# Last expert stage: one list per expert and choice, row weights in the tiles, and scatters that add to the output

## What is computed

```
x = x + L1_gnn(layernorm(x))                 # called x3 below
xf = layernorm(x).reshape(-1, 128)           # 8192 rows
top_w, top_i = top_k(xf @ Wg + bg, 2)
top_w = softmax(top_w)                       # 1/(1+e), e/(1+e) with e = exp(second - first)
for e in range(8):
    h = gelu(xf @ W1[e] + b1[e])             # 128 -> 512
    out += w_dense[:, e] * (h @ W2[e] + b2[e])
x = x + out
```

## Time and profile before

| quantity | us |
|---|---|
| three runs | 1516.81, 1512.54, 1510.47 |
| their median | 1512.54 |
| span of the profiled execution, first to last instruction | 1509.3 |
| phase_gnn1 with its barriers, about | 912 to 1188 |
| last expert stage, first transpose to last result | 1188.1 to 1457.5 |
| phase_finish, with the barrier before it | 1459 to 1509.3 |

### The profile page before, as it was taken

How to read it: one execution, slowest core, us unless ns; L and a number is a source line. 1 busy time by engine, 2 the same in 40 slices (tenths; PEclk the granted TensorE clock), 3 DMA queues, 4 the chain that set the end, 5 groups by cost and what they waited for, 6 DMA issues and landing times. The chain is left out here.

```text
span 1509.3 us, 31426 instructions
## 1 busy us (share of the span) xinstructions
PE 1158.0 (77%) x8464; PEld 980.3 (65%) x8464; DVE 935.4 (62%) x3451; ACT 727.7 (48%) x1776; POOL 772.8 (51%) x767
## 2 busy tenths in 40 slices
PE   5888888767888871799999983677762499999940
PEld 3666566557787761588888872555552389999930
DVE  3788888998888963355555554888865022222228
ACT  5777777537667751233333332544441245555520
POOL 3466666642666777344444441177776355555520
PEclk9999999979989985799999996988885699999985
DMA  7100000000011113466666662032212477777759
GB/s 186 22 2 2 2 1 2 2 1 1 30 33 36 35 44 89 145 197 196 195 193 193 194 194 88 29 99 69 68 43 71 142 223 228 229 228 227 225 168 288
DMA packets 133627, 166.82 MB, mean 111 GB/s; under 512 B 17328, under 2 KB 105136, under 8 KB 133520
## 3 DMA queue, kind: packets, MB, share of 16 engines
q1 hardware_dynamic: 99344, 122.30, 27.9%
q0 software_dynamic: 16832, 34.77, 6.5%
q10 hardware_dynamic: 17344, 8.49, 2.0%
HBM read 122.31 MB, written 43.19 MB: 110 GB/s over the span
## 5 line engine op out<-in xcount | busy, mean ns | idle before, releaser
L1879 POOL DMA_INDIRECT rows<-m_yb,m_dsti x270 | 258.7, 958 | 316.1 <-DVE m_dsti L2029 272.5
L1965 ACT ACTIVATE m_sg<-psum 128x256 f32<-128x256 f32 (+3 forms) x216 | 79.8, 370 | 179.1 <-PE psum L1909 132.9
L1110 POOL DMA_INDIRECT dispatch<-g_flat,g1r_pos x128 | 127.1, 993 | 58.0 <-issue 35.3
L1110 POOL DMA_INDIRECT dispatch<-common_v,a1r_pos x128 | 128.8, 1007 | 53.2 <-issue 40.2
L1909 PE MATMUL psum<-m_xT,m_w 128*128 128x256 f32 (+3 forms) x648 | 140.3, 366 | 0.7 <-ACT m_xT L1955 0.7
L1972 ACT ACTIVATE m_sg<-psum,m_w 128x256 f32<-128x256 f32 (+1 forms) x216 | 86.1, 458 | 93.9 <-PE psum L1914 93.2
L2011 DVE TENSOR_TENSOR m_hT<-psum,m_sg 128x256 f32<-128x256 f32 (+3 forms) x216 | 87.6, 407 | 62.4 <-ACT m_sg L1965 58.6
L1909 PEld LDWEIGHTS psum<-m_xT,m_w 128*128 128x128 f32 (+1 forms) x648 | 106.2, 178 | 18.3 <-ACT m_xT L1955 0.9
L1994 DVE TENSOR_TENSOR m_yb<-psum,m_w 128x256 f32<-128x256 f32 (+1 forms) x54 | 22.0, 407 | 144.8 <-PE psum L1924 144.8
L1924 PE MATMUL psum<-m_w,m_sg 128*128 128x128 f32 x808 | 99.2, 275 | 0.5 <-DVE m_yb L1994 0.5
L1914 PE MATMUL psum<-m_xT,m_w 128*128 128x256 f32 (+1 forms) x432 | 96.4, 366 | 0.5 <-ACT m_xT L1953 0.5
(11 more groups left out here) (273 smaller groups left out, 3056.1 us busy)
## 6 DMA issues: line engine op xcount, KB each, us to landing
m_w<-in_c_wall SPq DMA_DIRECT2D x54, 578.0 KB, 3.7
m_w<-in_c_wall SPq DMA_DIRECT2D x54, 533.0 KB, 3.5
m_xg<-dispatch SPq DMA_DIRECT2D x94, 130.0 KB, 3.6
ahead_w<-in_c_wall SPq DMA_DIRECT2D x18, 578.0 KB, 4.1
ahead_w<-in_c_wall SPq DMA_DIRECT2D x18, 533.0 KB, 4.5
g1c_y<-rows SPq DMA_DIRECT2D x32, 256.0 KB, 3.2
fin_y<-rows ACTq DMA_DIRECT2D x32, 256.0 KB, 6.4
rows<-m_yb,m_dsti POOLq DMA_INDIRECT x270, 3.3
```

The costliest lines, as they stand in the source:

```text
L1110: pool.indirect_dma_start(out=dest, out_offset=bass.IndirectOffsetOnAxis(ap=self.pos[t % 2][:, k, p:p + 1], axis=0), in_=flat[:, p, :], in ...
L1879: pool.indirect_dma_start(out=rows_out, out_offset=bass.IndirectOffsetOnAxis(ap=dsti[j][:, t:t + 1], axis=0), in_=yb[j][:, t, :], in_offse ...
L1965: act.activation(sg[j % 2][0:cn, k, 0:rows], up_banks[j % 2][k][0:cn, 0:rows], ACT.Silu)\
```

## The change

- The last mixture has 16 lists, one for each expert and choice, in two sets. The rank product, the positions, the base counts, the table and the tail fills have a leading dimension of 2. `Routing` and `Tables` get the new classes `SplitRouting` and `SplitTables` for this stage; the first mixture keeps the old ones.
- The number of tiles is fixed for each set: 31 full and 9 halves, so 80 tiles with 62 full and 18 halves in place of 72 with 63 and 9. All tiles of the first choice come first, then all of the second.
- ScalarE takes exp(second - first) once per batch inside the steps, writing it behind the row's id. `pool_scatter` waits for it. The key of the first expert is no longer written, the sum of both choices (`both`) no longer computed, and `vector_weights` no longer run for this stage.
- SP stores x3 to the output inside phase_gnn1, 16 stores of 256 KB, and waits for them at the stage's end. SP fills 16 list tails in place of 8, and 8 more spare tiles near the program's start.
- `phase_last` takes the place of the second `phase_experts` and of `phase_finish`. VectorE adds b2 and then multiplies each row by its weight; `yw_ready`, given by the second instruction, replaces `y_ready` for SP's loads and POOL's scatters. The scatter goes to the output with an add in the DMA. Before the first scatter of the second set POOL waits for all scatters of the first.
- The output tensor is longer by the place for the dummy rows; the host keeps the first 128 frames.

The diff, cut to its core:

```diff
+LISTS = 2 * (NE + 1)
+FULL_K = PAIRS * 128 // TILE - 1
+TILES_K = FULL_K + (PAIRS * 128 + NE * (HALF - 1)) // HALF - 2 * FULL_K
+OUT_FRAMES = FRAMES + TRASH // NODES
...
-            for rows in (list1, list2):
+            for rows, spare in ((list1, NE), (list2, NE), (list2, 2 * NE + 1)):
...
-        phase_experts(nc, banks, c, T, state2, list2, rows2, A["c_wall2"], False, "m2", x, None, None, ahead)
-        phase_finish(nc, x, state2, rows2, out_dram)
+        T2 = SplitTables(ctx, nc)
+        phase_gnn1(nc, W, x, banks, c, T2, state, rows1, list2, ahead, A["c_wall2"], out_dram)
+        phase_last(nc, banks, c, T2, list2, out_rows, A["c_wall2"], ahead)
...
+class SplitRouting:
...
+        r = self.ranks(bank)
+        pe.matmul(r[:, :, 0:PB, :], self.c["tri"][:, :], self.oh[:, :, :, :], start=True, stop=False, skip_group_check=True)
...
+    def scalar_exp(self, act, t, flat):
...
+        act.wait_ge(*self.d_ready.now(t))
+        act.activation(flat[:, :, C + 1], self.d[:, t % 2, :], ACT.Exp).then_inc(self.e_ready.sem, 1)
...
+    def pool_tag(self, pool, t, flat):
...
+        pool.wait_ge(*self.step.now(t, 0))
+        pool.tensor_copy(flat[:, :, C], self.c["ids"][:, bass.ds(t * PB, PB)]).then_inc(self.tagged.sem, 1)
...
+    def pool_scatter(self, pool, t, first, last, flat, dest):
...
+        pool.wait_ge(*self.pstep.now(t, 4))
+        pool.wait_ge(*self.e_ready.now(t))
+        pool.wait_ge(*self.tagged.now(t))
...
+class SplitTables:
...
+        sp.wait_ge(self.chain, 1)
+        for k in range(2):
+            for e in range(NE):
+                row = sp.value_load(self.tail[0:1, k, e:e + 1], min_val=0, max_val=(LISTS - 1) * CAP)
+                sp.dma_start(rows_in[bass.ds(row, TILE), :].rearrange("(t p) c -> p t c", t=2), nobody[:, 2 * e:2 * e + 2, :])\
+                  .then_inc(self.filled, 16)
...
                     mixed_out(g)
+                    if b % 2 == 1 and runs_batch(h - 1):
+                        R.scalar_exp(act, h - 1, flat[(h - 1) % 3])
                     head_h3(g + 1)
                 in_pairs(step)
-                R.scalar_exp(act, False)
...
-                turns(sp, 0, GROUPS // 2, lambda turn: M.fetch(sp, turn))
+                def store_x3(g):
+                    sp.wait_ge(*x3_ready.now(g))
+                    sp.dma_start(out_dram[:, PG * g:PG * g + PG, :], x[:, PG * g:PG * g + PG, :]).then_inc(x3_stored, 16)
+
+                for turn in range(GROUPS // 2):
+                    M.fetch(sp, turn)
+                    for g in range(2 * turn - 6, 2 * turn - 4):
+                        if g >= 0:
+                            store_x3(g)
+                for g in range(GROUPS - 6, GROUPS):
+                    store_x3(g)
                 T.sync(sp, c, dest)
                 ahead.sync(sp, "m2", T, R, wall, dest)
+                sp.wait_ge(x3_stored, 16 * GROUPS)
...
+def phase_last(nc, banks, c, T, rows_in, out_rows, wall, ahead):
...
+                    sp.wait_ge(*yw_ready.now(g, j - UN))
...
+                        pool.wait_ge(*yw_ready.now(g, j))
+                        pool.wait_ge(*share_ready.now(g, 4 * j + 3))
+                        pool.sem_inc(gate, 1)
+                        if isinstance(g, int) and g == SIDE and j == 0:
+                            for i in range(UN):
+                                pool.wait_ge(stored[i], sent(SIDE, i))
+                        for t in range(halves(g, j)):
+                            pool.indirect_dma_start(
+                                out=out_rows, out_offset=bass.IndirectOffsetOnAxis(ap=dsti[j][:, t:t + 1], axis=0),
+                                in_=yb[j][:, t, :], in_offset=None, compute_op=ALU.add).then_inc(stored[j], 16)
...
+                    dve.tensor_tensor(y, bY[:, 0:n * C].rearrange("r (t c) -> r t c", t=n),
+                                      bass.AP(b.tensor, b.offset, [b.ap[0], [0, n], [1, C]]), ALU.add).then_inc(y_ready.sem, 1)
+                    dve.wait_ge(*y_ready.now(g, j))
+                    dve.wait_ge(*share_ready.now(g, 4 * j + 2))
+                    dve.tensor_tensor(y, y, over_c(share[jj][:, 0:n], n), ALU.mult).then_inc(yw_ready.sem, 1)
...
+                    dve.tensor_scalar(total[j][:, 0:n], xg[j][:, 0:n, C + 1], 1.0, None, ALU.add).then_inc(sr.sem, 1)
+                    dve.wait_ge(*sr.now(g, 4 * j))
+                    dve.reciprocal(share[j][:, 0:n], total[j][:, 0:n]).then_inc(sr.sem, 1)
+                    if k == 1:
+                        dve.wait_ge(*sr.now(g, 4 * j + 1))
+                        dve.tensor_tensor(share[j][:, 0:n], share[j][:, 0:n], xg[j][:, 0:n, C + 1], ALU.mult).then_inc(sr.sem, 1)
+                    else:
+                        dve.sem_inc(sr.sem, 1)
+                    dve.tensor_copy(dsti[j][:, 0:n], xg[j][:, 0:n, C]).then_inc(sr.sem, 1)
```

More of the change, by code:

```diff
@@ L1804, in phase_experts @@
         sg = [sb(f"sg{i}", [128, NK, TILE]) for i in range(2)]
[L1805 removed]
+        hT = [sb(f"hT{i}", [128, NK, TILE]) for i in range(2)]
         dst = [sb(f"dst{i}", [128, 2]) for i in range(UN)]
@@ L2004, in body @@
                         rows = HALF * halves(g, j)
-                        if late is not None and adds:
+                        if adds:
                             late_add(g, j)
-                        if swiglu:
-                            for k, (c0, cn) in enumerate(chunks):
-                                dve.wait_ge(*act_done.now(g, NK * j + k))
-                                dve.wait_ge(*pe_down.now(g, j - 2))
-                                dve.tensor_tensor(hT[j % 2][0:cn, k, 0:rows], up_banks[j % 2][k][0:cn, TILE:TILE + rows],
-                                                  sg[j % 2][0:cn, k, 0:rows], ALU.mult).then_inc(h_ready.sem, 1)
+                        for k, (c0, cn) in enumerate(chunks):
+                            dve.wait_ge(*act_done.now(g, NK * j + k))
+                            dve.wait_ge(*pe_down.now(g, j - 2))
+                            dve.tensor_tensor(hT[j % 2][0:cn, k, 0:rows], up_banks[j % 2][k][0:cn, TILE:TILE + rows],
+                                              sg[j % 2][0:cn, k, 0:rows], ALU.mult).then_inc(h_ready.sem, 1)
                         if not (first and j == 0):
@@ L2418, in _ @@
                 in_pairs(step)
-                T.vector(dve, c, state2["base"], R.pstep.now(GROUPS // 2 - 1, 4))
-                R.vector_weights(dve, False)
+                T.vector(dve, c, R.pstep.now(GROUPS // 2 - 1, 4))
             @block.gpsimd
@@ L2464, in _ @@
             @block.vector
             def _(dve):
-                open_signals(dve, M.dve_signals)
-        with nc.Block() as block:
-            @block.scalar
-            def _(act):
-                M.fetch(act, 0)
-                turns(act, 1, GROUPS // DEPTH, lambda turn: M.fetch(act, turn))
-            @block.vector
-            def _(dve):
-                turns(dve, 0, GROUPS // DEPTH, lambda turn: [M.vector_mix(dve, turn * DEPTH + b, b, x) for b in range(DEPTH)])
-            @block.sync
-            def _(sp):
-                def body(g):
-                    sp.wait_ge(*M.mixed.now(g, 2 * PG - 1))
-                    sp.dma_start(out_dram[:, bass.ds(g * PG, PG), :], x[:, bass.ds(g * PG, PG), :]).then_inc(stored, 16)
-                turns(sp, 0, GROUPS, body)
-                sp.wait_ge(stored, 16 * GROUPS)
+                open_signals(dve, [y_ready, yw_ready, share_ready])
@@ L2487, with body @@
+                def body(g, k):
+                    for j in range(UN):
+                        if not (isinstance(g, int) and g == 0 and j == 0):
+                            out(g, side(g - 1) if isinstance(g, int) and j == 0 else k, j - 1)
+                        row_share(g, k, j)
+                all_turns(dve, body)
+                out(TURNS - 1, 1, UN - 1)
+        clear_taken(nc)
 _INS = ['x', 'adj', 'L0_gnn_w_qkv', 'L0_gnn_ln1_g', 'L0_gnn_ln1_b', 'L0_gnn_ln2_g', 'L0_gnn_ln2_b', 'L0_gnn_w1',
```

451 lines of the change are left out of this document (388 added, 63 removed).

## The result

The changed kernel takes 1541.41 us by the median of four runs (1534.03 to 1546.65), the kernel before beside it 1513.39: a ratio of 1.0171, interval 1.0131 to 1.0212. The ratios of this document are those on record with their intervals; they are not the quotients of the two medians, which would be 1.0185 here. A second measurement of the same kernel, as a control among the experiments, gave 1527.58 against 1511.65: 1.0094, interval 1.0059 to 1.0128. Both are slower by more than the 0.5% that the prediction took for telling; whether the first is slower by over 2% its interval leaves open. Both lie in the range of 1499 to 1545, and both lie above the forecast of 1513 and its own range of 1503 to 1523.

The account below looks back on a forecast made before the run. No engine was full; TensorE paced full tiles, DMA half tiles, VectorE's combining and fetches the end, POOL and VectorE alternated in phase_gnn1. -44.9 + 25.4 + 1 + 7 + 4 + 8 = +0.5: 1513 us, range 1499 to 1545.

Parts of the forecast that it names:

- rival 2: Last expert stage: adding scatters make POOL the bound; 1548 us at twice the plain scatter time, chance 0.16.
- The end: After the last result: one product, scatter and landing replace the 52.1 us tail, leaving 7.2 us; -44.9 us.
- Tiles and switch: Last expert stage: one full tile fewer, nine half tiles more, +25.4 us; switch between sets, +1 us.
- The loads: Last expert stage: SP's loads wait for the multiplied result and land later; +7 us in full tiles, +4 in half tiles.
- So there is 0.47 us of slack.: Full tiles: rows land at 1306.2 for a transpose at 1306.67; the new product takes that slack.
- Bounds are thus none and 3.5.: Last expert stage: extra DMA engine-us for a scatter's add; upper taken, giving a DMA share of 0.85.
- the prediction's halving: Full tiles: load lateness reaches the pace by half, as a buffer comes round once in four tiles; 0.12 us a tile.
- POOL's issue: Last expert stage: adding scatters take up to 1.5 us of POOL's busy time each, staying covered; 0 us.
- phase_gnn1: In phase_gnn1: POOL's wait for ScalarE's exp passes some 1.2 us through per pair of steps; +8 us, bounds 0 and +12.
- Stores, tail fills, row products: x3 stores in phase_gnn1, eight more tail fills on SP, VectorE's small row products: covered or in idle time, 0 us.
- Rival 1: Expert stage and phase_gnn1: loads stay in time and POOL catches up; -17.5 us, 1495 us, chance 0.25.
- Rival 3: Last expert stage: adding scatters hold DMA engines, landings come 0.7 us later; 1532 us, chance 0.14.

Follow-up runs that it names:

- plain_and_loads: Changed kernel with scatters storing instead of adding and loads released by the result, not its product: 1507.5 us, ratio 0.9960 to the kernel before.
- split_loads: Changed kernel with each tile's rows loaded ahead of its weights, on a semaphore of their own: 1507.4 us, ratio 0.9959 to the kernel before.
- before_split: Kernel before, with rows loaded ahead of weights in its last expert stage: 1509.4 us, ratio 0.9958 to the kernel before.
- before_waits_outputs: Kernel before, with POOL's first scatter of each phase_gnn1 batch also waiting for ScalarE's four outputs: 1523.7 us, ratio 1.0060.
- all_three: Changed kernel with exp ahead of the transposed copy, loads released by the result, rows loaded ahead of weights: 1497.8 us, ratio 0.9901 to the kernel before.
- plain_scatter: Changed kernel with its scatters storing instead of adding: 1513.9 us, ratio 0.9998 to the kernel before.

## Why the prediction was right and wrong

The range held, the forecast did not. No change was forecast, and 0.9 and 1.7% more were measured, an outcome with a chance of 0.33. That 1541 lay inside is in part luck: the range went up to 1545 for the sake of rival 2, POOL as the bound, and the runs show late loads in its place.

**The end: right.** -44.9 forecast, -43.4 measured. The tail is 8.7 us for a forecast of 7.2: the last scatter stands behind the one before it, 1.69 us after the result where the forecast had 1.44, and is itself 0.6 us longer. No run shows the 1.5 us for closing the program by itself. From the start of the last scatter to the end it is 7.0 us, and 6.1 in plain_and_loads, where the forecast had 4.3 + 1.5.

**Tiles and switch: right.** 26.4 forecast, 25.6 measured in plain_and_loads, where both latenesses are gone. Two small errors offset each other in it: nine half tiles and the switch took 27.9 us (1323.49 to 1355.20, less one full tile) for 9 x 3.24 + 1 = 30.2, and 60 full tiles at 3.79 us in place of 3.76 took 1.6 more.

**The loads: the step that failed.** The term for full tiles was mis-sized. I put 0.12 us a tile and +7 us on it, and +4 on the half tiles. Against plain_and_loads the four executions with the unchanged stage lost 316.2 - 294.6 = 21.6 us. Between the first and the last results of the full tiles it is (4.08 - 3.79) x 60 = 17 us: 4.08 is (4.11 + 4.06 + 4.00 + 4.09 + 4.19 + 4.11 + 4.04 + 4.03)/8, 3.79 the mean of plain_and_loads' two sets. The other 4 lie at the half tiles, as forecast. The mechanism was the one described, as split_loads shows; three sizes were off.

- "So there is 0.47 us of slack." I took the slack up to the transpose at 1306.67. The rows enter TensorE with the weight load in front of it, which the trace of before has at 1306.46: slack 0.26. And that was for a landing at the median: in some tiles there was none, as before_split shows.
- The loads came not 0.45 us later but 1.74 - 1.19 = 0.55, since the product starts 0.13 behind the result that it waits for.
- "Bounds are thus none and 3.5." The add was 10.7 - 2.6 = 8 engine-us, and the share 0.91, not 0.85. The landing in the full tiles rose from 3.6 us by the median to 3.9, by 0.3 and not by 0.2, so this error cost little.

With these sizes the prediction's halving gives (0.55 - 0.26 + 0.3)/2 = 0.30 us a tile, 18 us for 60, near the 17 measured. That fits; no run tests the halving by itself.

The Trainium skill (Collectives: The Full Stack, on why ReduceScatter is half of AllGather) has two read descriptors for an add where a copy has one. By that rule, taken over from collectives to a scatter as an estimate, an adding scatter would cost twice a plain one. This case's packets go from 31 to 139 and its engine time from 2.6 to 10.7 us; the measurement decides, and it is four times.

**POOL's issue: right by a hair.** I allowed up to 1.5 us of busy time and named 1.58 as the threshold; it was 1.554. No row stood behind the 1.5, so that it came out just under the threshold is luck. It cost nothing that shows as long as the loads were late, and it fills POOL once they are not.

**phase_gnn1: right in mechanism, a little small.** +8 forecast, 9 to 12 by three pairs of kernels and by before_waits_outputs. The prediction's own numbers (a start at 1114.18 in place of 1112.53, of which 0.33 is free) give 1.3 us a pair of steps, 9 in all, where it wrote 1.2. The remaining 8 us of the first profiled execution came together with a lower clock there; that the clock is their cause is not shown. What I did not do was to ask how early the exp's operand is ready: that question shows the repair in the same trace.

**Stores, tail fills, row products: right** at 0 within what can be told. With the exp early the phase takes 208.3 to 209.2 us, in before and before_split it took 209.6 and 203.8.

**The rivals.** Rival 1 (covered waits, 1495) is near what all_three made of it, with 1497.8, but only with the exp early and with an order of loads that gains in the kernel before too. The change by itself did not do it. Rival 3 (loads later, 1532) was nearest to the truth: late loads in most full tiles, though with 0.3 us more of landing and not its 0.7. My 0.45 for the forecast rested on a slack read off one tile.

## What to carry to other kernels

Read the slack of a transfer at the first instruction that reads its data (the weight load, not the product), and over many tiles: the gaps between results show lateness that a busy share of 169.63 in 170 us hides, small as it was there. When a wait is added behind a small operation, look how early its operand was ready, and where in the other engine's list there is a gap before the waiter needs it. Before two loads share one semaphore, ask which is needed first: with rows ahead of weights, and a semaphore for each, the cost of a later release and of slower landings was gone.

## What was not expected of the hardware

- A scatter that adds costs POOL 1554 ns in place of 957 and the DMA engines 10.7 us in place of 2.6, with 139 packets in place of 31.
- At a DMA share of 0.91 the fetches of rows landed 3.9 us after issue by the median, 0.2 later than in plain_scatter at 0.71. all_three held a pace of 3.75 and 3.71 us a full tile at a share of 0.98.
- Rows that were issued ahead of the weights landed 2.8 us after issue in place of 4.0.
- The same phase of the same kernel took 219.7 and 228.2 us in two executions, with TensorE busy for 124.3 and 132.3 us at a granted clock of 0.72 and 0.68. A stage that leaves TensorE idle in between should be compared over several executions before a theory is put on it. All thirteen executions together did part the kernels with the late exp from those without.
